# A fused window-attention, linear-attention and expert kernel: another order on all engines, three filler pairs per group instead of twelve

## The chip, the cores and the metric

The kernel runs on one core of a Trainium2 chip. The core has a matmul engine (PE, TensorE), three engines for the rest (DVE, VectorE; ACT, ScalarE; POOL, GpSimd) and SP, which issues DMAs. Each engine works through its own instructions in their order, and they wait for each other by semaphores. The metric is device microseconds of one execution, lower is better. Three runs of the kernel before took 11870.49, 11959.04 and 12028.54 us; the median is 11959.04.

## What is computed

The reference takes x of shape (32, 56, 56, 64) through three layers:

```python
x = _L0_conv_ref(x, ...)      # Swin block: LN, shifted 7x7 windows, 8 heads with bias and mask, projection,
                              # then LN, 64 -> 256 gelu, LN, 256 -> 64, both with residuals
t = _to_tokens(x)
t = t + _L1_attn_ref(_ln_t(t), ...)   # linear attention: k and v normed per head, kv = k^T v / HW,
                                      # q @ kv, projection, gelu, residual
t = t + _L1_ffn_ref(_ln_t(t), ...)    # softmax router, top 2 of 8 experts, 64 -> 256 gelu -> 64 each
```

## The kernel before, in words

The input is cut into 256 groups of 392 tokens (4 tiles of two 7x7 windows, 98 tokens each); eight groups make an image, over which the linear attention sums. Everything is one software pipeline. An iteration handles a different step of many groups at once: each engine has a list `ORDER[engine]` of `step:offset`, and in iteration n it executes the step for group n + offset. Offsets such as +2, +1, 0 belong to the window attention and its MLP, -1 to -2 to the linear attention's sums, -9 to -12 to its second pass and the router, and -24 to -27 to the experts. These work on tiles of 128 tokens that chose the same pair of experts; tokens are scattered to HBM by POOL and loaded again by SP, three tiles per iteration (271 iterations' worth). Behind the 256th group only the later offsets still run.

What a step name is on PE, with its line: `zT`, `oT`, `z2T`, `xnT`, `uT` four transposes each (L603); `q` L626, `k` L634, `v` L642; `s0` to `s3` attention scores of one tile (L650); `pT0` to `pT3` transposed probabilities (L658); `o0` to `o3` probabilities times values (L669); `proj` L683; `fc10`, `fc11` L695; `hT0`, `hT1` L704; `fc2` L714; `kv` L727; `G` L734; `lp` L766; `logit` L779; `rk` L787 to L791; `tx` L801; `ei0` to `ei2` the experts' first layer in f16 (L820); `eo0` to `eo2` their second layer (L829 the bias, L834). An f32 matmul shows as two records in the profile.

PE has eight banks of results, ps0 to ps7 (letters A, O, P, S, B, H, K, Y). Before a step writes a bank, `handed_on` waits until whoever read the bank's former content is done; the table `HANDED` holds, for each step, these signals in the order in which they can be expected.

A filler is a step whose name begins with f: `fK0`, `fP0` and so on, with the bank's letter. It is `keep_warm` (L609 to L615), two f16 matmuls of 128 x 512 whose results nobody reads:

```python
            def keep_warm(name, bank):
                handed_on(pe, name)
                for _ in range(2):
                    pe.matmul(bank[:, :], identh[:, :], we1[0][:, 0:512], start=True, stop=True)
```

They run only for the 256 groups, in `fK0 fP0 fS0 fK1 fY0 fA0 fK2 fS1 fB0 fY1 fP1 fH0`.

Of the kernel before, what the change touches and what calls it, by code (L numbers as in the profile page):

```python
# [80 lines left out]
def build(nc, x, cst, wqkv, bqkv, table, projw, projb, fc1w, fc1b, fc2w, fc2b, amask, rel, lnvecs, ln3,  # L81
# [12 lines left out]
    with ExitStack() as ctx:  # L94
# [263 lines left out]


        ORDER = dict(  # L360
            pe="""tx:-26 q:+2 fK0:+0 s0:+2 pT1:+1 o0:+1 s1:+2 z2T:+0 o1:+1 ei0:-26 lp:-10 fP0:+0 pT2:+1 mix0:+0 fc10:+0
                  mix1:+0 fS0:+0 s2:+2 ei1:-26 fc11:+0 mix2:+0 o2:+1 pT3:+1 xnT:-10 fK1:+0 mix3:+0 uT:-1 logit:-10 s3:+2
                  v:+2 hT0:+0 ei2:-26 fY0:+0 o3:+1 fA0:+0 hT1:+0 mix4:+0 fK2:+0 kv:-1 eo0:-26 oT:+1 fS1:+0 fB0:+0 eo1:-26
                  zT:+3 eo2:-26 proj:+1 fc2:+0 fY1:+0 fP1:+0 fH0:+0 k:+3 rk:-10 pT0:+2 G:-1""",
            dve="""u:-1 t2:-10 mix0:+0 oj0:+1 stx:-10 mix1:+0 mvx:-10 cx:-10 sa:-11 xn:-10 sb2:+2 mx1:+2 mix2:+0 rt0:-10
                   sb3:+2 c1:+3 tw:-11 rt1:-10 rt2:-10 z:+3 rt3:-10 st30:+0 mix3:+0 pa:-11 li:-11 rc0:+1 oj1:+1 mx2:+2
                   on0:+1 rc1:+1 rt4:-10 mx3:+2 rt5:-10 on1:+1 rt6:-10 st31:+0 rt7:-10 kvss:-1 rt8:-10 rt9:-10 mv1:+4
                   w:-11 mv3:+0 kve:-1 yv:-26 rt10:-10 rt11:-10 rt12:-10 kvr:-1 x1:+1 cd:-10 tr:+0 pk:-10 t:+0 st2:+1
                   kvn:-1 stu:+0 sl:-11 mv2:+1 Gsum:-1 c2:+1 sp:-10 qbd:+3 st1:+5 z2:+1 ya:-26 ct:-10 sb0:+3 ys:-26 sb1:+3
                   mx0:+3 mvu:+0 lo:-10 cu:+0""",  # L370
            act="""sd:-2 exp:+1 ke:+2 xc:-26 pt0:+1 pt1:+1 tanh:-11 om0:+1 z2t:+0 h00:-26 lpg:-10 pt2:+1 h01:-26 h02:-26
                   ge0:+0 h03:-26 h10:-26 utc:-9 ge1:+0 pt3:+1 xnt:-10 h11:-26 h12:-26 utk:-1 h13:-26 om1:+1 h20:-26
                   hi:-10 h21:-26 hnt0:+0 hnt1:+0 h22:-26 ve:+2 h23:-26 sq:-1 ot:+1 zt:+3""",
            pool="""pw3:-1 r2:+0 pw2:+0 r1:+3 ri:-27 sc0:-12 dm00:-12 dm10:-13 dm20:-14 dm30:-15 dm40:-16 dm50:-17
                    dm60:-18 x1b:+0 ru:-1 pwu:-1 pw1:+3 sc1:-12 dm01:-12 dm11:-13 dm21:-14 dm31:-15 dm41:-16 dm51:-17
                    dm61:-18 so0:-27 rx:-10 pwx:-10 sub0:+2 v0:-10 tu:-2 tk:-9 so1:-27 v1:-10 sc2:-12 dm02:-12 dm12:-13
                    dm22:-14 dm32:-15 dm42:-16 dm52:-17 dm62:-18 sub1:+2 sub2:+2 sc3:-12 dm03:-12 dm13:-13 dm23:-14
                    dm33:-15 dm43:-16 dm53:-17 dm63:-18 so2:-27 r3:+0 sub3:+2""",
            sp="""x:+6 tl:-25 tz:-25 ls:-12 wl:-24""",
        )  # L380

        HANDED = dict(
            fA0="uT_kept.0:-1 hid_ready.1:+0 z2T_ready.0:+0 q_ready.0:+2 x1_ready.0:+0 zT_ready.0:+2 oT_ready.0:+0 hnT_ready.1:-1",
            q="x1_ready.0:+0 zT_ready.0:+2 oT_ready.0:+0 hnT_ready.1:-1 uT_kept.0:-2 hid_ready.1:-1 z2T_ready.0:-1 q_ready.0:+1",
            z2T="q_ready.0:+2 x1_ready.0:+0 zT_ready.0:+2 oT_ready.0:+0 hnT_ready.1:-1 uT_kept.0:-2 hid_ready.1:-1 z2T_ready.0:-1",
            fc11="z2T_ready.0:+0 q_ready.0:+2 x1_ready.0:+0 zT_ready.0:+2 oT_ready.0:+0 hnT_ready.1:-1 uT_kept.0:-2 hid_ready.1:-1",
            uT="hid_ready.1:+0 z2T_ready.0:+0 q_ready.0:+2 x1_ready.0:+0 zT_ready.0:+2 oT_ready.0:+0 hnT_ready.1:-1 uT_kept.0:-2",
            hT1="uT_kept.0:-1 hid_ready.1:+0 z2T_ready.0:+0 q_ready.0:+2 x1_ready.0:+0 zT_ready.0:+2 oT_ready.0:+0 hnT_ready.1:-1",
            oT="hnT_ready.1:+0 uT_kept.0:-1 hid_ready.1:+0 z2T_ready.0:+0 q_ready.0:+2 x1_ready.0:+0 zT_ready.0:+2 oT_ready.0:+0",
            zT="oT_ready.0:+1 hnT_ready.1:+0 uT_kept.0:-1 hid_ready.1:+0 z2T_ready.0:+0 q_ready.0:+2 x1_ready.0:+0 zT_ready.0:+2",  # L390
            proj="zT_ready.0:+3 oT_ready.0:+1 hnT_ready.1:+0 uT_kept.0:-1 hid_ready.1:+0 z2T_ready.0:+0 q_ready.0:+2 x1_ready.0:+0",
            fB0="hnT_ready.0:+0 logit_ready.0:-10 xnT_ready.0:-10 hid_ready.0:+0 gelu_ready.0:-10 spot_ready.0+count_ready.0:-11 fc2_scaled.0:-1",
            lp="spot_ready.0+count_ready.0:-11 fc2_scaled.0:-1 hnT_ready.0:-1 logit_ready.0:-11 xnT_ready.0:-11 hid_ready.0:-1 gelu_ready.0:-11",
            fc10="gelu_ready.0:-10 spot_ready.0+count_ready.0:-11 fc2_scaled.0:-1 hnT_ready.0:-1 logit_ready.0:-11 xnT_ready.0:-11 hid_ready.0:-1",
            xnT="hid_ready.0:+0 gelu_ready.0:-10 spot_ready.0+count_ready.0:-11 fc2_scaled.0:-1 hnT_ready.0:-1 logit_ready.0:-11 xnT_ready.0:-11",
            logit="xnT_ready.0:-10 hid_ready.0:+0 gelu_ready.0:-10 spot_ready.0+count_ready.0:-11 fc2_scaled.0:-1 hnT_ready.0:-1 logit_ready.0:-11",
            hT0="logit_ready.0:-10 xnT_ready.0:-10 hid_ready.0:+0 gelu_ready.0:-10 spot_ready.0+count_ready.0:-11 fc2_scaled.0:-1 hnT_ready.0:-1",
            fc2="hnT_ready.0:+0 logit_ready.0:-10 xnT_ready.0:-10 hid_ready.0:+0 gelu_ready.0:-10 spot_ready.0+count_ready.0:-11 fc2_scaled.0:-1",
            rk="fc2_scaled.0:+0 hnT_ready.0:+0 logit_ready.0:-10 xnT_ready.0:-10 hid_ready.0:+0 gelu_ready.0:-10 spot_ready.0+count_ready.0:-11",
            fK0="g_ready.0:-2 kv_ready.0:-2 mix3:-1 mix2:-1 mix1:-1 mix0:-1",  # L400
            fK1="mix2:+0 mix1:+0 mix0:+0 g_ready.0:-2 kv_ready.0:-2 mix3:-1",
            fK2="mix3:+0 mix2:+0 mix1:+0 mix0:+0 g_ready.0:-2 kv_ready.0:-2",
# [14 lines left out]
            v="pT_ready.3:+1 pT_ready.2:+1 pT_ready.1:+1 pT_ready.0:+1 vexp_ready.0:+1",
            pT0="vexp_ready.0:+2 pT_ready.3:+1 pT_ready.2:+1 pT_ready.1:+1 pT_ready.0:+1",
            fS0="score_bias.1:+2 score_bias.0:+2 score_bias.3:+1 score_bias.2:+1",
            fS1="score_bias.3:+2 score_bias.2:+2 score_bias.1:+2 score_bias.0:+2",  # L420
# [1254 lines left out]
```

How the kernel before makes its waits and increments, by code:

```python
        def now(eng, name, n, t=0, alone=None):  # L282
            if isinstance(n, int) and (n < 0 or COUNTS[name] * n + t + 1 <= 0):
                return
            eng.wait_ge(S[name], COUNTS[name] * n + (t + 1))
            if alone:
                eng.sem_inc(held[alone], 1)
# [151 lines left out]
        def handed_on(eng, name):  # L441
            for entry in HANDED[name].split():
                signals, at = entry.split(":")
                at = int(at)
                if signals[:3] == "mix":
                    if runs_at("mix", ran["like"] + at, 0):
                        eng.wait_ge(mix_dve, 5 * (ran["image"] if ran["like"] % GROUPS + at >= 0 else ran["image"] - 1)
                                    + MIX_DONE[int(signals[3])])
                        return
                    continue
                parts = signals.split("+")
                last = STEPS if parts[0].split(".")[0] in ("xs_ready", "yv_ready", "h_ready") else TOTAL
                if ran["like"] + at in range(last):
                    for part in parts:
                        signal, t = part.split(".")
                        now(eng, signal, ran["n"] + at, int(t))
                    return
# [56 lines left out]
        @block.sync  # L516
        def _(sp):
            for dst, src in SETUP_LOADS:
                sp.dma_start(dst, src).then_inc(setup, 16)
            sp.wait_ge(setup_dve, 9)
            for w in range(2):
                sp.dma_start(pos[w * WA:(w + 1) * WA, :], pos1).then_inc(setup_pos, 16)
```

## Time and profile before

| | before |
|---|---|
| median of three runs | 11959.04 us (11870.49 to 12028.54) |
| the profiled execution | 11922.89 us, its span 11921.1 us |
| granted TensorE clock, mean of the span | 0.769 |
| PE busy | 10713.8 us, 90% |
| DVE, ACT, POOL busy | 6277.7, 5532.9, 5262.0 us |
| filler matmuls (L615) | 6144, 2237.0 us busy |

The busy time of PE counts from the start of a matmul to its modelled end, and matmuls overlap, so a busy PE is not PE at its peak. The granted clock is the share of TensorE's full 2.4 GHz; it has two levels here, 1.00 and 0.50, and a value between is a mean over both.

### The profile page before, as it was taken

How to read it: one execution, taken by the hardware profiler on the slowest of the kernel's cores; microseconds unless marked ns; L12 is line 12 of the kernel's file. 1: busy time of each engine (PE TensorE's matmuls, PEld its weight loads, DVE VectorE, ACT ScalarE, POOL GpSimd, SP SyncE). 2: the span in 40 equal slices, each digit the busy share in tenths (PEclk: the TensorE clock that was granted, in tenths of full speed). 3: DMA queues.
4: the chain of work that ended last, by engine and by line, in shares of the span. 5: the costliest groups of instructions: out<-in, count | busy, mean ns of one | idle time of the engine just before them, and what ended most of it. 6: DMA issues, size and time to landing. Idle time of an engine off the chain costs nothing. (4 is left out here: it accounts for less than half of the span.)

```text
span 11921.1 us, 262791 instructions
## 1 busy us (share of the span) xinstructions
PE 10713.8 (90%) x67913; PEld 7893.3 (66%) x67913; DVE 6277.7 (53%) x26878; ACT 5532.9 (46%) x12487; POOL 5262.0 (44%) x7260
## 2 busy tenths in 40 slices
PE   7899999999999999999999999999999999999655
PEld 5666666666666666666666667666666666666544
DVE  5666555555555565655555555555555555555200
ACT  3545444445544454544445454445445444454211
POOL 2444444444544444544444454444444444454321
PEclk9878777778877787877778787778878877787555
...
GB/s 20 7 9 14 14 16 16 15 15 16 17 15 15 15 16 16 16 16 16 15 16 16 16 16 16 15 16 17 16 16 16 16 16 15 16 16 14 21 19 10
DMA packets 222504, 184.37 MB, mean 15 GB/s; under 512 B 63337, under 2 KB 193331, under 8 KB 220552
## 3 DMA queue, kind: packets, MB, share of 16 engines
...
## 5 line engine op out<-in xcount | busy, mean ns | idle before, releaser
L615 PE MATMUL ps<-we_hi,identh 128*128 128x512 f16 x6144 | 2237.0, 477 | 36.9 <-DVE yv L1304 35.9
L1605 ACT ACTIVATE ht<-ps,be 128x128 f32<-128x128 f32 x3252 | 1109.7, 369 | 1212.7 <-PE ps L820 758.1
L1364 POOL TENSOR_TENSOR sc<-sc,mx 98x392 f32<-98x392 f32 x1024 | 860.3, 840 | 1756.4 <-DVE mx L1012 1743.6
...
L1427 POOL DMA_INDIRECT slots<-rec,slot x1024 | 1072.4, 1047 | 356.1 <-issue 225.2
L650 PE MATMUL ps<-kexp,qbd 128*98 128x392 f32 x2048 | 1134.7, 643 | 75.1 <-DVE qbd L999 52.8
L834 PE MATMUL ps<-we,ht 128*128 x6504 | 1181.5, 340 | 0.0
L834 PEld LDWEIGHTS ps<-we,ht 128*128 128x128 f32 x6504 | 1053.3, 246 | 132.1 <-issue 73.3
L1513 ACT ACTIVATE first<-ps,cs 98x144 f32<-98x144 f32 x512 | 194.6, 380 | 2020.7 <-PE ps L669 2020.7
L1454 POOL DMA_INDIRECT out_y<-ys,row_at x813 | 838.8, 1032 | 592.4 <-DVE ys L1316 245.9
L820 PE MATMUL ps<-xs,we_hi 128*128 128x128 f16 x3252 | 699.6, 251 | 405.9 <-issue 271.6
L669 PEld LDWEIGHTS ps<-vexp,pt 98*98 98x98 f32 x8192 | 974.7, 191 | 99.4 <-issue 28.6
L615 PEld LDWEIGHTS ps<-we_hi,identh 128*128 128x128 f16 x6144 | 663.8, 122 | 492.7 <-issue 254.3
L669 PE MATMUL ps<-vexp,pt 98*98 98x36 f32 x8192 | 955.1, 267 | 0.0
L1495 ACT ACTIVATE kexp<-ps,cs 128x196 f32<-128x196 f32 x2048 | 672.0, 440 | 478.5 <-PE ps L634 472.8
L695 PE MATMUL ps<-wf,z2t 65*98 65x256 f32 x2048 | 650.9, 447 | 252.4 <-ACT rec L1575 251.1
L1006 DVE TENSOR_TENSOR sc<-ps,bias 98x392 f32<-98x392 f32 x1024 | 574.6, 561 | 530.9 <-PE ps L650 530.2
L820 PEld LDWEIGHTS ps<-xs,we_hi 128*128 x3252 | 357.6, 110 | 724.5 <-issue 623.0
L1353 POOL TENSOR_TENSOR rs<-ve,cs 98x4 f32<-98x4 f32 x768 | 781.9, 1018 | 70.1 <-issue 49.6
L1480 ACT ACTIVATE pt<-ps 98x392 f32<-98x392 f32 x1024 | 514.1, 502 | 567.4 <-PE ps L658 560.4
L820 PE MATMUL ps<-xs,we_lo 128*128 128x128 f16 x3252 | 694.6, 244 | 0.4
L1097 DVE TENSOR_SCALAR kvse<-kvsd 98x128 f32<-98x128 f32 x256 | 58.6, 229 | 1177.7 <-ACT kvsd L1570 1177.7
...
## 6 DMA issues: line engine op xcount, KB each, us to landing
...
xg<-in_x SPq DMA_DIRECT2D x256, 98.0 KB
...
lw<-tile_list SPq DMA_DIRECT2D x271, 0.0 KB
...
tile_list<-entry SPq DMA_DIRECT2D x64, 0.5 KB
```

Of the source, the lines that this page charges most:

```text
L615: pe.matmul(bank[:, :], identh[:, :], we1[0][:, 0:512], start=True, stop=True)
L650: pe.matmul(pS[0:TOK, 0:HEADS * WA], qbd[:, t, :], kexp[:, t, :], start=True, stop=True)\
L669: last = pe.matmul(o[:, :, 2 * h:2 * h + 2, :], pt[:, t % 2, h, :], vexp[:, 2 * t:2 * t + 2, 2 * h:2 * h + 2, :], start=True, stop=True)
L695: last = pe.matmul((pB, pA)[half][0:TOK, (t % 2) * HID:(t % 2 + 1) * HID], z2t_[:, cols(t)], wf1[:, :], start=True, stop=True)
L820: last = pe.matmul(pH[:, 128 * (2 * e + h):128 * (2 * e + h + 1)], we1[half][:, bass.ds(pair[e] * HID + 128 * h, 128)], xs[:, q, :], start ...
L834: last = pe.matmul(dst, ht[:, q, 2 * e + h, :], we2[:, bass.ds(chosen[q][e] * 2 + h, 1), :].rearrange("p a c -> p (a c)"), start=False, st ...
L1353: pool.tensor_tensor(rs[L][:, :, :], ve[L][:, :, :], k("minushalf")[0:TOK].unsqueeze(1).to_broadcast([TOK, ve[L].shape[1], GT]), ALU.pow)\
L1364: pool.tensor_tensor(s, s, mx[:, t, :].unsqueeze(2).to_broadcast([TOK, HEADS, WA]), ALU.subtract)\
L1427: pool.indirect_dma_start(slots, bass.IndirectOffsetOnAxis(ap=slot[:, j % 2, t:t + 1], axis=0), rec[:, bass.ts(j % RB, 1), t, :].rearrange ...
L1454: pool.indirect_dma_start(out, bass.IndirectOffsetOnAxis(ap=row_at[:, q:q + 1], axis=0), ys[:, bass.ts(j % 2, 1), q, :].rearrange("p a c - ...
L1495: last = act.activation(kexp[:, :, WA * h:WA * (h + 1)], keys_, ACT.Copy, scale=k("headmask")[:, h:h + 1])
L1605: act.activation(ht[:, q, b, :], pH[:, 128 * b:128 * (b + 1)], ACT.Gelu, bias=be1[:, bass.ds(chosen[q][b // 2] * 2 + b % 2, 1)], scale=1.0 ...
```

## The change

Only the tables `ORDER` and `HANDED` are different. Nine of the twelve filler steps are gone (`fH0`, `fS0`, `fB0` stay), and the steps of all four computing engines stand in another order; some move to the neighbouring iteration, which changes their offset. No operation of the computation is added or removed. SP's list is the same. Lines below the tables stand 9 lines higher. Of the PE list and of HANDED:

```diff
-            pe="""tx:-26 q:+2 fK0:+0 s0:+2 pT1:+1 o0:+1 s1:+2 z2T:+0 o1:+1 ei0:-26 lp:-10 fP0:+0 pT2:+1 mix0:+0 fc10:+0
+            pe="""mix0:+0 tx:-26 fH0:+0 zT:+2 v:+1 mix1:+0 lp:-10 fS0:+0 q:+2 k:+2 pT0:+1 fB0:+0 rk:-11 z2T:+0 ei0:-26
...
-            fH0="h_ready.11:-26 h_ready.7:-26 h_ready.3:-26",
+            fH0="h_ready.11:-27 h_ready.7:-27 h_ready.3:-27",
```

The whole order on PE in an iteration is now: mix0 tx fH0 zT v mix1 lp fS0 q k pT0 fB0 rk z2T ei0 s0 pT1 mix2 fc10 fc11 o0 s1 ei1 o1 xnT mix3 s2 uT pT2 logit ei2 o2 hT0 pT3 kv hT1 o3 eo0 s3 eo1 eo2 mix4 oT fc2 proj G. It was: tx q fK0 s0 pT1 o0 s1 z2T o1 ei0 lp fP0 pT2 mix0 fc10 mix1 fS0 s2 ei1 fc11 mix2 o2 pT3 xnT fK1 mix3 uT logit s3 v hT0 ei2 fY0 o3 fA0 hT1 mix4 fK2 kv eo0 oT fS1 fB0 eo1 zT eo2 proj fc2 fY1 fP1 fH0 k rk pT0 G.

The first place on PE is behind fc2. In the kernel before (L714 is fc2, L615 the fillers, L634 k, L787 to L791 rk):

```order
L683 MATMUL ps<-wp,ot 98x64 x4
L714 MATMUL ps<-wf,hnt 98x64 x8
L615 MATMUL ps<-we_hi,identh 128x512 x6
L634 MATMUL ps<-zt,wa 64x196 x2
L787 MATMUL ps<-count,onesf 128x140
```

In the changed kernel (L705 is fc2, L674 proj, L725 G, L792 tx, L606 the filler pair fH0, L594 zT, L633 v):

```order
L705 MATMUL ps<-wf,hnt 98x64 x8
L674 MATMUL ps<-wp,ot 98x64 x4
L725 MATMUL ps<-kvn 65x65 x4
L287 ISA
L792 MATMUL ps<-identh,rt 128x128 x3
L606 MATMUL ps<-we_hi,identh 128x512 x2
L287 REGISTER_ALU
L594 MATMUL ps<-cs,z 64x98 x4
L633 MATMUL ps<-wa,zt 98x64 x8
```

Three filler pairs in a row became one, and it stands behind proj, G and tx.

The second place is around s0. In the kernel before (L626 q, L650 s0, L658 pT1, L669 o0):

```order
L801 MATMUL ps<-identh,rt 128x128 x3
L626 MATMUL ps<-zt,wq 64x196 x2
L615 MATMUL ps<-we_hi,identh 128x512 x2
L650 MATMUL ps<-kexp,qbd 98x392
L658 MATMUL ps<-cs,pr 98x98 x4
L669 MATMUL ps<-vexp,pt 98x2x18 x4
```

In the changed kernel, from the pair fB0 on (L778 to L782 rk, L594 z2T, then ei0, of which the first matmul is shown; its last, s0 (L641), pT1 and fc10 and fc11 (L686) follow behind the "..."):

```order
L606 MATMUL ps<-we_hi,identh 128x512 x2
L778 MATMUL ps<-count,onesf 128x140
L780 MATMUL ps<-pick,before 128x112
...
L594 MATMUL ps<-cs,z 64x98 x4
...
L811 MATMUL ps<-xs,we_lo 128x128
L641 MATMUL ps<-kexp,qbd 98x392
L649 MATMUL ps<-cs,pr 98x98 x4
L686 MATMUL ps<-wf,z2t 98x256 x4
```

No filler stands between q and s0 any more; rk, z2T and ei0 stand between the pair and s0.

## Rows read from the trace of the kernel before

**Rows 1.** The page: span, and busy time of each engine with its share and instructions.
```profile
span 11921.1 us, 262791 instructions
PE 10713.8 (90%) x67913; PEld 7893.3 (66%) x67913; DVE 6277.7 (53%) x26878; ACT 5532.9 (46%) x12487; POOL 5262.0 (44%) x7260
```

**Rows 2.** Busy time by stretch; L650's and L615's alone (PE, PEld, PEclk, DMA).
```profile
core 0: us, PE busy (x) PEld busy (x) DVE busy (x) ACT busy (x) POOL busy (x), PEclk, DMA share, GB/s
5000.00:7000.00 2000.00, 1865.37 (x11915) 1368.88 (x11914) 1109.94 (x4778) 973.05 (x2193) 926.81 (x1282) 0.78 0.06 16
11000.00:11921.00 921.00, 543.43 (x2621) 430.68 (x2620) 125.67 (x541) 182.48 (x588) 241.39 (x303) 0.50 0.07 17
...
5000.00:7000.00 2000.00, 203.73 (x368) 60.54 (x368) 0.78 0.06 16
...
11000.00:11921.00 921.00, 0.00 (x0) 0.00 (x0) 0.50 0.07 17
```

**Rows 3.** Single groups by stretch, from proj to proj (columns as in rows 2).
```profile
1108.00:1143.60 35.60, 32.25 (x263) 24.14 (x262) 23.53 (x100) 21.07 (x49) 20.52 (x29) 1.00 0.07 18
4066.90:4124.30 57.40, 53.30 (x263) 38.87 (x262) 23.57 (x100) 22.31 (x49) 19.88 (x28) 0.55 0.05 12
10314.10:10370.80 56.70, 53.27 (x262) 38.82 (x262) 23.59 (x100) 22.28 (x49) 19.91 (x28) 0.55 0.04 12
```

**Rows 4.** Waits, 5000 to 7000 us: who waited for whom, total, times, longest.
```profile
PE ps L695 <- ACT rec L1575: 46.2, 41, 1.2
PE ps L820 <- issue: 25.1, 27, 1.0
```

**Rows 5.** Timeline of PE: start, us, what; full level first, then low, then pairs.
```profile
6047.85 1.55 PE L714 MATMUL ps<-wf,hnt 128*98 128x64 f32 x16
6049.23 1.46 PE L615 MATMUL ps<-we_hi,identh 128*128 128x512 f16 x6
...
6013.08 2.77 PE L615 MATMUL ps<-we_hi,identh 128*128 128x512 f16 x6
...
6001.21 0.60 PE L615 MATMUL ps<-we_hi,identh 128*128 128x512 f16 x2
...
6054.76 1.03 PE L615 MATMUL ps<-we_hi,identh 128*128 128x512 f16 x2
```

**Rows 6.** Stretches around a fall of the clock (as rows 2), then PE's timeline there.
```profile
6003.40:6009.20 5.80, 5.80 (x44) 4.62 (x43) 3.65 (x21) 4.23 (x11) 3.29 (x6) 1.00 0.10 28
6009.40:6016.00 6.60, 6.60 (x32) 4.67 (x33) 5.18 (x24) 3.75 (x4) 0.65 (x1) 0.50 0.14 37
6016.20:6026.00 9.80, 9.16 (x82) 6.38 (x78) 6.12 (x24) 5.68 (x15) 5.49 (x9) 1.00 0.03 7
...
6007.82 0.48 PE L829 MATMUL ps<-b2pair,onesf 1*128 x2
6008.24 1.10 PE L834 MATMUL ps<-we,ht 128*128 x8
6009.18 1.44 PE L683 MATMUL ps<-wp,ot 65*98 65x64 f32 x8
6010.41 2.87 PE L714 MATMUL ps<-wf,hnt 128*98 128x64 f32 x16
```

**Rows 7.** L615 in 3 us before each rise; then all of those 355 us.
```profile
5989.20:5992.20 3.00, 1.06 (x2) 0.30 (x2) 0.50 0.10 28
...
6340.80:6343.80 3.00, 1.06 (x2) 0.17 (x2) 0.50 0.10 28
sum 36.00, PE 20.69 PEld 5.44; mean PE 1.72 PEld 0.45
...
5988.80:6343.80 355.00, 334.65 (x2100) 244.20 (x2098) 195.34 (x846) 171.25 (x388) 164.28 (x229) 0.77 0.06 16
```

**Rows 8.** A stretch at the low level: L615 in it, and its row behind fc2.
```profile
6111.70:6169.70 58.00, 12.03 (x24) 3.25 (x24) 0.50 0.06 14
...
6144.43 2.74 PE L615 MATMUL ps<-we_hi,identh 128*128 128x512 f16 x6 [1.26 <-DVE yv L1304]
```

More of the change, by code:

```diff
@@ L360, in build @@
         ORDER = dict(
-            pe="""tx:-26 q:+2 fK0:+0 s0:+2 pT1:+1 o0:+1 s1:+2 z2T:+0 o1:+1 ei0:-26 lp:-10 fP0:+0 pT2:+1 mix0:+0 fc10:+0
[L362 to L378, printed above, removed]
+            pe="""mix0:+0 tx:-26 fH0:+0 zT:+2 v:+1 mix1:+0 lp:-10 fS0:+0 q:+2 k:+2 pT0:+1 fB0:+0 rk:-11 z2T:+0 ei0:-26
+                  s0:+2 pT1:+1 mix2:+0 fc10:+0 fc11:+0 o0:+1 s1:+2 ei1:-26 o1:+1 xnT:-10 mix3:+0 s2:+2 uT:-1 pT2:+1
+                  logit:-10 ei2:-26 o2:+1 hT0:+0 pT3:+1 kv:-1 hT1:+0 o3:+1 eo0:-26 s3:+2 eo1:-26 eo2:-26 mix4:+0 oT:+1
+                  fc2:+0 proj:+1 G:-1""",
@@ new lines, in build @@
+            dve="""mix0:+0 tr:-1 mv2:+0 c2:+0 mix1:+0 cd:-11 t:-1 stu:-1 pk:-11 mvu:-1 qbd:+2 z2:+0 t2:-10 stx:-10 mvx:-10
+                   st1:+4 sp:-11 c1:+3 ct:-11 cx:-10 sa:-11 sb0:+2 xn:-10 cu:-1 tw:-11 mx0:+2 z:+3 mv1:+4 sb1:+2 st30:+0
+                   mix2:+0 mx1:+2 sl:-11 u:-1 w:-11 st31:+0 mv3:+0 rt0:-10 oj0:+1 rt1:-10 pa:-11 li:-11 rt2:-10 rc0:+1
+                   rt3:-10 mix3:+0 rt4:-10 sb2:+2 on0:+1 kvss:-1 mx2:+2 rt5:-10 rt6:-10 rt7:-10 rt8:-10 oj1:+1 sb3:+2
+                   rc1:+1 mx3:+2 rt9:-10 kve:-1 on1:+1 rt10:-10 lo:-10 kvr:-1 yv:-26 kvn:-1 ya:-26 x1:+1 Gsum:-1 rt11:-10
+                   st2:+1 ys:-26 rt12:-10""",
@@ new lines, in build @@
+            act="""om1:+0 hnt1:-1 sd:-2 ot:+0 exp:+1 xc:-26 zt:+2 tanh:-11 ve:+1 lpg:-10 ke:+2 pt0:+1 z2t:+0 h00:-26
+                   utc:-9 h01:-26 pt1:+1 h02:-26 ge0:+0 h03:-26 h10:-26 h11:-26 ge1:+0 xnt:-10 om0:+1 h12:-26 h13:-26
+                   utk:-1 pt2:+1 hi:-10 h20:-26 hnt0:+0 h21:-26 pt3:+1 h22:-26 h23:-26 sq:-1""",
+            pool="""ri:-27 sub3:+1 pw3:-1 sc0:-12 dm00:-12 dm10:-13 dm20:-14 dm30:-15 dm40:-16 dm50:-17 dm60:-18 tu:-3
+                    r2:+0 pw2:+0 so0:-27 sc1:-12 dm01:-12 dm11:-13 dm21:-14 dm31:-15 dm41:-16 dm51:-17 dm61:-18 ru:-1
+                    rx:-10 pwx:-10 pwu:-1 tk:-11 r1:+4 v0:-10 sc2:-12 dm02:-12 dm12:-13 dm22:-14 dm32:-15 dm42:-16
+                    dm52:-17 dm62:-18 sub0:+2 so1:-27 v1:-10 r3:+0 sc3:-12 dm03:-12 dm13:-13 dm23:-14 dm33:-15 dm43:-16
+                    dm53:-17 dm63:-18 pw1:+4 so2:-27 sub1:+2 x1b:+0 sub2:+2""",
@@ L382, in build @@
         HANDED = dict(
[L383 to L402, printed above, removed]
+            zT="x1_ready.0:+0 oT_ready.0:+0 hnT_ready.1:-1 uT_kept.0:-2 hid_ready.1:-1 z2T_ready.0:-1 q_ready.0:+1 zT_ready.0:+1",
@@ new lines, in build @@
+            q="zT_ready.0:+2 x1_ready.0:+0 oT_ready.0:+0 hnT_ready.1:-1 uT_kept.0:-2 hid_ready.1:-1 z2T_ready.0:-1 q_ready.0:+1",
+            z2T="q_ready.0:+2 zT_ready.0:+2 x1_ready.0:+0 oT_ready.0:+0 hnT_ready.1:-1 uT_kept.0:-2 hid_ready.1:-1 z2T_ready.0:-1",
+            fc11="z2T_ready.0:+0 q_ready.0:+2 zT_ready.0:+2 x1_ready.0:+0 oT_ready.0:+0 hnT_ready.1:-1 uT_kept.0:-2 hid_ready.1:-1",
+            uT="hid_ready.1:+0 z2T_ready.0:+0 q_ready.0:+2 zT_ready.0:+2 x1_ready.0:+0 oT_ready.0:+0 hnT_ready.1:-1 uT_kept.0:-2",
@@ new lines, in build @@
+            hT1="uT_kept.0:-1 hid_ready.1:+0 z2T_ready.0:+0 q_ready.0:+2 zT_ready.0:+2 x1_ready.0:+0 oT_ready.0:+0 hnT_ready.1:-1",
+            oT="hnT_ready.1:+0 uT_kept.0:-1 hid_ready.1:+0 z2T_ready.0:+0 q_ready.0:+2 zT_ready.0:+2 x1_ready.0:+0 oT_ready.0:+0",
+            proj="oT_ready.0:+1 hnT_ready.1:+0 uT_kept.0:-1 hid_ready.1:+0 z2T_ready.0:+0 q_ready.0:+2 zT_ready.0:+2 x1_ready.0:+0",
+            fB0="gelu_ready.0:-10 fc2_scaled.0:-1 hnT_ready.0:-1 logit_ready.0:-11 xnT_ready.0:-11 hid_ready.0:-1 spot_ready.0+count_ready.0:-12",
@@ new lines, in build @@
+            lp="fc2_scaled.0:-1 hnT_ready.0:-1 logit_ready.0:-11 xnT_ready.0:-11 hid_ready.0:-1 spot_ready.0+count_ready.0:-12 gelu_ready.0:-11",
+            rk="gelu_ready.0:-10 fc2_scaled.0:-1 hnT_ready.0:-1 logit_ready.0:-11 xnT_ready.0:-11 hid_ready.0:-1 spot_ready.0+count_ready.0:-12",
+            fc10="spot_ready.0+count_ready.0:-11 gelu_ready.0:-10 fc2_scaled.0:-1 hnT_ready.0:-1 logit_ready.0:-11 xnT_ready.0:-11 hid_ready.0:-1",
+            xnT="hid_ready.0:+0 spot_ready.0+count_ready.0:-11 gelu_ready.0:-10 fc2_scaled.0:-1 hnT_ready.0:-1 logit_ready.0:-11 xnT_ready.0:-11",
@@ L403, in build @@
+            logit="xnT_ready.0:-10 hid_ready.0:+0 spot_ready.0+count_ready.0:-11 gelu_ready.0:-10 fc2_scaled.0:-1 hnT_ready.0:-1 logit_ready.0:-11",
+            hT0="logit_ready.0:-10 xnT_ready.0:-10 hid_ready.0:+0 spot_ready.0+count_ready.0:-11 gelu_ready.0:-10 fc2_scaled.0:-1 hnT_ready.0:-1",
+            fc2="hnT_ready.0:+0 logit_ready.0:-10 xnT_ready.0:-10 hid_ready.0:+0 spot_ready.0+count_ready.0:-11 gelu_ready.0:-10 fc2_scaled.0:-1",
             mix0="g_ready.0:-2 kv_ready.0:-2 mix3:-1 mix2:-1 mix1:-1 mix0:-1",
@@ L408, in build @@
             G="kv_ready.0:-1 mix3:+0 mix2:+0 mix1:+0 mix0:+0 g_ready.0:-2",
+            k="o_joined.1:+0 o_joined.0:+0 kexp_ready.0:+1",
             o0="kexp_ready.0:+2 o_joined.1:+0 o_joined.0:+0",
             o2="o_joined.0:+1 kexp_ready.0:+2 o_joined.1:+0",
-            k="o_joined.1:+1 o_joined.0:+1 kexp_ready.0:+2",
-            fP0="pT_ready.1:+1 pT_ready.0:+1 vexp_ready.0:+1 pT_ready.3:+0 pT_ready.2:+0",
-            fP1="vexp_ready.0:+2 pT_ready.3:+1 pT_ready.2:+1 pT_ready.1:+1 pT_ready.0:+1",
+            v="pT_ready.3:+0 pT_ready.2:+0 pT_ready.1:+0 pT_ready.0:+0 vexp_ready.0:+0",
+            pT0="vexp_ready.0:+1 pT_ready.3:+0 pT_ready.2:+0 pT_ready.1:+0 pT_ready.0:+0",
             pT1="pT_ready.0:+1 vexp_ready.0:+1 pT_ready.3:+0 pT_ready.2:+0 pT_ready.1:+0",
@@ L416, in build @@
             pT3="pT_ready.2:+1 pT_ready.1:+1 pT_ready.0:+1 vexp_ready.0:+1 pT_ready.3:+0",
[L417 to L420, printed above, removed]
+            fS0="score_bias.3:+1 score_bias.2:+1 score_bias.1:+1 score_bias.0:+1",
             s0="score_bias.3:+1 score_bias.2:+1 score_bias.1:+1 score_bias.0:+1",
@@ L424, in build @@
             s3="score_bias.2:+2 score_bias.1:+2 score_bias.0:+2 score_bias.3:+1",
-            fY0="xs_ready.0:-26 yv_ready.0:-27",
-            fY1="yv_ready.0:-26 xs_ready.0:-26",
             tx="yv_ready.0:-27 xs_ready.0:-27",
             eo0="xs_ready.0:-26 yv_ready.0:-27",
-            fH0="h_ready.11:-26 h_ready.7:-26 h_ready.3:-26",
+            fH0="h_ready.11:-27 h_ready.7:-27 h_ready.3:-27",
             ei0="h_ready.11:-27 h_ready.7:-27 h_ready.3:-27",
```

## The prediction

> **What bounds the kernel now.** I read the page first, then the steady stretch, then single groups. The page [rows 1] gives 11921.1 us of span, PE busy 90% of it, DVE 53%, ACT 46%, POOL 44%. From about 1000 to 11000 us the kernel repeats one pattern: [rows 2] show 368 score matmul records (L650, 8 for a group) in 2000 us, so 46 groups, 43.5 us for a group, at a granted clock of 0.78. Behind 11000 us only the experts' tail is left (921 us), at 0.50.
>
> That 0.78 is a mean of two levels: 1.00 is 2.4 GHz, 0.50 is 1.2 GHz. I write s for the share of time at the full level; 0.78 is s = 0.57. [rows 3] put single groups beside each other, cut from one `proj` (L683) to the next. At clock 1.00 a group takes 35.6 us; at 0.55 (s = 0.10) two of them take 57.4 and 56.7 us. In these low groups PE is busy 53.3 us, DVE 23.6, ACT 22.3, POOL 19.9: nobody but PE is near the bound. Even in the full group the others have 12 us to spare (23.5, 21.1, 20.5 of 35.6), while PE is busy 32.3. So PE sets the pace at both levels, and what a group costs is PE's work divided by its clock. The waits between engines [rows 4] are small on PE: the longest, fc1 behind the gelu on ACT, is 46.2 us in 46 groups, 1.0 us each.
>
> **The change, part by part.** Three things happen: 18 of 24 filler matmuls (L615) go from each group; all steps stand in another order; the waits that went with the fillers go with them.
>
> *Fillers.* Six of them in a row take 1.46 us at the full level and two take 0.60 [rows 5], so one costs (1.46 - 0.60) / 4 = 0.215 us. At the low level six take 2.77 and two 1.03: (2.77 - 1.03) / 4 = 0.435 us. Eighteen are 3.9 us at full and 7.8 us at low. They write banks that are overwritten and nobody reads; DVE, ACT and POOL lose nothing. At the low level all of the 7.8 us is on the path, since PE is busy 93% there. At full, up to the same 3.9 us; if the fillers only covered waits that now open, as little as 0.
>
> *The new order.* The same operations on each engine; every step of a group is still there. On PE I looked for a step put right behind the one it waits for. fc2 now stands between oT and proj and covers the copy of ot; z2T has ei0, s0 and pT1 before fc10; v uses the zT of a group before. No place looks worse than the one of now. I cost the reordering at 0 us, with 1.0 us for a group either way (the longest PE wait of [rows 4] taken away or doubled), 250 us over the run.
>
> *Were the clock to stay as it is*, that would be all: at s = 0.57 about 0.57 x 3.9 + 0.43 x 7.8 = 5.6 us less for a group if all counts.
>
> *The clock.* It does not stay by itself: what PE executes decides it. In [rows 6] PE has no idle time at all from 6003.4 to 6009.2 us, at 1.00, and still the clock is 0.50 from 6009.4 on. What PE does there are the experts' second layer (L829, L834), two transposes (L603), then proj: many weight loads with 64 to 98 columns each, and bias matmuls with one active row. Then six fillers run at the low level, and from 6016.2 us the clock is 1.00 again. The same stretch of steps one group later, 6045 to 6051 [rows 5], stayed at full.
>
> How the clock comes back is shown by [rows 7]: I took the 3 us before each of the 12 rises between 5989 and 6344 us. Every one holds fillers: five hold six of them, one four, six two; the fillers are busy 20.69 of the 36 us. The stretch that never rose is as telling: 58 us from 6111.7 to 6169.7 at 0.50, with all 24 fillers in it [rows 8]; its triple came behind a wait of 1.26 us on yv. The pairs that stand alone beside transposes or small matmuls did not lift the clock.
>
> In the new order there is no triple and no double any more (the first pair of order pieces in the section on the change): fc2 is followed by proj, G and tx, then one pair. Nor does a pair stand directly beside a score matmul (s) or an expert's first layer (ei), as fK0 before s0, fS0 before s2 and fY0 behind ei2 do now (the second pair of pieces shows the first of them): rk and z2T stand between fB0 and ei0. What is left that is dense in full-size matmuls is one place: ei0 followed directly by s0.
>
> The Trainium skill (TensorE: Matmul & The Clock Gate, section "Why this matters for your kernels") puts it as a matter of idle gaps: keep TensorE busy without gaps between bursts and it keeps its clock. By that rule, with PE nearly as busy after the change as now, the clock would stay, and the time would be that of the third rival below. The trace disagrees: the drop of rows 6 falls into a stretch without any gap. The same page says in its Part 4 that transposes do not count as activity in the way of other matmuls; that fits the drop, and it speaks against an order in which transposes and small matmuls stand alone.
>
> **The sum.** One line through the groups. Low: the mean of 57.4 and 56.7 is 57.05 at s = 0.10; full: 35.6 at s = 1. Slope (57.05 - 35.6) / 0.9 = 23.8, so 59.4 us at s = 0. After: 59.4 - 7.8 = 51.6 at s = 0 and 35.6 - 3.9 = 31.7 at s = 1, or P = 51.6 - 19.9 s. The line gives 45.8 for the kernel of now at s = 0.57, where 43.5 was measured: it lies up to 2.3 us high in the middle and little near the ends. Break-even with 43.5 is at s = 0.41, a granted clock of 0.70.
>
> What is s after? Now: 12 rises in 355 us, 8.2 groups, so 1.5 rises for a group; at clock 0.77, s = 0.54 [rows 7], the full stretches are 355 x 0.54 / 12 = 16 us long each. After: none of the 12 had a filler-free cover, and one moderately dense place for a group is left. I take one rise in two groups (my choice, between 0 and 1), and stretches of 14 us, a bit shorter, since the fillers that carried PE over its waits are gone. s = 0.5 x 14 / 49 = 0.14, granted clock 0.57. P = 51.6 - 2.8 = 48.8; half a microsecond off for the line's bulge: 48.3. That is 4.8 us more than 43.5, on about 250 groups (256, the first few run in the ramp): +1200 us. The ramp before and the tail behind have the same work, and the tail has no fillers [rows 2]: 0. The last is 11921 + 1200 = 13120; with what lies around the span (11922.89 against 11921.1) and the roundings I say **13100 us**. The profiled execution is 0.3% under the median of the runs shown (11959.04), within their spread of 11870 to 12029.
>
> **Rivals.**
> - *The clock stays almost always low* (s under 0.05): the one dense place is not enough. P = 51.6 to 50.6, say 51.3: +7.8 x 250 = 1950, 13,870 us. For it: the stretch of 58 us in rows 8 with all its fillers. Chance 0.18.
> - *The clock falls only to about 0.70* (s = 0.36 to 0.46): nearly two rises for a group in stretches of 10 us. P near 43.5, 11,650 to 12,150 us, no change. Chance 0.08.
> - *Faster: the clock stays where it is.* Were s 0.57, P = 51.6 - 11.3 = 40.3 by the line and 43.5 - 5.6 = 37.9 by subtraction; 11,921 - 250 x 3.2 = 11,120 down to 10,520 us. It decides from s = 0.46 on. The mechanism would be that s and ei, with 128 active rows each, hold the clock by themselves. For it: the group keeps all eight s records of 392 columns and 24 ei matmuls of 128. Against it: [rows 6, 7]. Chance 0.09. The Trainium skill's rule on idle gaps (page and section as above) would have it so too.
> - *The waits open.* At full, the fillers covered waits, so 3.9 us come back as idle. At s = 0.14 that is 0.14 x 3.9 = 0.5 us for a group, +140 us; it moves nothing by itself, but idle PE time at full makes the next fall earlier. It is in the upper half of the forecast's range.
>
> **The numbers.** Forecast (s between 0.05 and 0.36) 0.65, always low 0.18, same 0.08, faster 0.09. A change of 2% is about what a measurement of this kernel can tell from no change (its three runs lie 1.3% apart). Slower by over 2%: 0.83; same 0.08; faster 0.09. The range leaves out faster, same and the far end of low: from s = 0.33 (P = 45.0, +1.5 x 250 = 380: 12,300 us) to s near 0 (P = 51.4, +7.9 x 250 = 1980: 13,900 us).
>
> **What would show it.** In the profile after, the steady stretch should have PE still over 90% busy, a granted clock of 0.52 to 0.62, fewer groups in 2000 us (about 41 instead of 46), L615 with a quarter of its records, and stretches of 50 us and more at 0.50. Fillers at full should still cost 0.215 us each. DVE, ACT and POOL should have the same busy time for a group. If the clock is at 0.75 or above, the step on the clock is wrong and the kernel is faster; if it is at 0.55 and the group takes over 52 us, the new order has waits at the low level that I costed at 0; if the group at full takes over 34 us, the fillers covered waits.

## The result and the profile after

The changed kernel takes 12502.32 us (median of 4 runs, 12440.77 to 12611.87) against 11952.26 us of the kernel before beside it: a ratio of 1.047, 95% interval 1.036 to 1.058. It is slower, as forecast, and inside the range of 12,300 to 13,900 us; but the forecast was 13,100, +1200 us for the span, and the span grew by 12454.0 - 11921.1 = 533 us. The size was wrong by more than a factor of two. The ratios and their intervals, here and in the table of experiments, leave out executions that took over 1.5% more than the fastest of the same kernel; the medians are of all.

The page of the changed kernel, span and busy time of each engine, beside [rows 1]:

```profile
span 12454.0 us, 253288 instructions
PE 11746.4 (94%) x63305; PEld 9438.6 (76%) x63305; DVE 6529.8 (52%) x26878; ACT 5623.8 (45%) x12487; POOL 5294.9 (43%) x7260
```

PE has 4608 matmuls less and is busy 1033 us longer. Its steady stretch, then two groups from proj to proj, then PE's stretches around one rise and one fall (busy time by stretch, columns as in [rows 2]):

```profile
5000.00:7000.00 2000.00, 1960.42 (x10683) 1578.99 (x10683) 1110.73 (x4586) 951.84 (x2106) 894.65 (x1229) 0.60 0.06 15
2960.30:3009.60 49.30, 49.30 (x244) 40.16 (x243) 27.68 (x115) 22.01 (x49) 20.34 (x28) 0.50 0.05 14
4836.10:4880.80 44.70, 43.72 (x245) 35.32 (x244) 24.16 (x100) 21.71 (x49) 20.37 (x28) 0.61 0.06 15
4880.80:4898.00 17.20, 17.20 (x95) 13.06 (x95) 9.35 (x51) 9.77 (x22) 7.19 (x10) 0.52 0.02 5
4898.20:4908.20 10.00, 9.12 (x71) 6.76 (x69) 7.14 (x31) 4.39 (x13) 5.75 (x9) 0.97 0.05 16
4908.80:4925.00 16.20, 16.20 (x75) 14.19 (x74) 7.72 (x19) 6.37 (x12) 7.03 (x9) 0.50 0.11 25
```

The granted clock of the steady stretch is 0.60 where it was 0.78. A group wholly at 1.2 GHz takes 49.3 us, in all of which PE is busy; a common group takes 44.7 us and holds one piece of some 10 us at 2.4 GHz. The timeline of PE shows where that piece begins and ends. At the low level stand ei0 (L811) and directly behind it s0 (L641); the transposes pT1 (L649) behind them are already faster (0.72 us; 0.50 is the full level). Towards the end stand logit (L770) and a gap before ei2 (L811). The matmuls of ei2 still take 0.22 to 0.23 us; o2 (L660) and hT0 (L695) behind it are slow again:

```profile
4895.32 0.31 PE L811 MATMUL ps<-xs,we_hi 128*128 128x128 f16 x1
4895.43 0.31 PE L811 MATMUL ps<-xs,we_lo 128*128 128x128 f16 x1
4895.54 1.57 PE L641 MATMUL ps<-kexp,qbd 128*98 128x392 f32 x2
4896.90 0.72 PE L649 MATMUL ps<-cs,pr 98*98 98x98 f32 x4
...
4903.95 0.50 PE L594 MATMUL ps<-cs,u 98*64 98x98 f32 x4 [0.35 <-ACT hid L1534]
4904.28 0.50 PE L649 MATMUL ps<-cs,pr 98*98 98x98 f32 x4
4904.71 0.85 PE L770 MATMUL ps<-wrt,xnt 64*98 64x8 f32 x8
4906.07 0.23 PE L811 MATMUL ps<-xs,we_hi 128*128 128x128 f16 x1 [0.50 <-issue]
...
4907.20 1.17 PE L660 MATMUL ps<-vexp,pt 98*98 98x36 f32 x8
4908.17 0.90 PE L695 MATMUL ps<-cs,hid 98*128 98x98 f32 x4
```

No filler pair stands at either end of this piece. The trace says how common it is: of 134 rises between 1000 and 9000 us, 118 have ei0 directly followed by s0 in the 3 us before them, and 130 of 133 falls have the ei2 behind logit there. The three pairs are almost never near a rise: in 9 of the 134 the pair fH0 stands in those 3 us, in the others none. PE's waits, by place (5000 to 7000 us: total, times, longest), are the counterpart of [rows 4]:

```profile
PE ps L811 <- issue: 16.1, 34, 0.6
PE ps L594 <- ACT hid L1534: 10.7, 31, 0.4
PE ps L792 <- issue: 7.4, 6, 1.5
```

The wait of fc1 for the gelu, 46.2 us before, is gone, and no wait of that size took its place.

### The profile page after: what moved, and what is told of

It is laid out like the page before. It is cut to its first block and busy times, and to the rows that moved or that the text cites. A ratio compares the mean times of both kernels' runs of the same rounds, so it can differ in the third digit from the quotient of the medians.

```text
span 12454.0 us, 253288 instructions
## 1 busy us (share of the span) xinstructions
PE 11746.4 (94%) x63305; PEld 9438.6 (76%) x63305; DVE 6529.8 (52%) x26878; ACT 5623.8 (45%) x12487; POOL 5294.9 (43%) x7260
## 5 line engine op out<-in xcount | busy, mean ns | idle before, releaser
L825 PE MATMUL ps<-we,ht 128*128 x6504 | 1582.6, 424 | 0.0
L825 PEld LDWEIGHTS ps<-we,ht 128*128 128x128 f32 x6504 | 1430.9, 324 | 180.2 <-issue 177.7
L641 PE MATMUL ps<-kexp,qbd 128*98 128x392 f32 x2048 | 1317.4, 738 | 12.0 <-issue 6.9
L660 PEld LDWEIGHTS ps<-vexp,pt 98*98 98x98 f32 x8192 | 1166.1, 228 | 112.1 <-issue 38.3
L660 PE MATMUL ps<-vexp,pt 98*98 98x36 f32 x8192 | 1181.5, 302 | 23.0 <-DVE first L1011 9.3
L811 PE MATMUL ps<-xs,we_hi 128*128 128x128 f16 x3252 | 767.7, 268 | 358.6 <-issue 199.2
L649 PEld LDWEIGHTS ps<-cs,pr 98*98 98x98 f32 x4096 | 597.5, 180 | 334.2 <-issue 334.0
L811 PEld LDWEIGHTS ps<-xs,we_hi 128*128 x3252 | 378.9, 117 | 618.0 <-issue 509.3
L606 PE MATMUL ps<-we_hi,identh 128*128 128x512 f16 x1536 | 791.9, 617 | 6.6 <-ACT rec L1566 6.6
L649 PE MATMUL ps<-cs,pr 98*98 98x98 f32 x4096 | 774.0, 334 | 0.0
L811 PE MATMUL ps<-xs,we_lo 128*128 128x128 f16 x3252 | 753.1, 262 | 2.0
L705 PE MATMUL ps<-wf,hnt 128*98 128x64 f32 x4096 | 714.3, 365 | 0.0
L705 PEld LDWEIGHTS ps<-wf,hnt 128*98 128x98 f32 x4096 | 707.4, 288 | 0.0
```

Source lines behind the costliest of these rows:

```text
L641: pe.matmul(pS[0:TOK, 0:HEADS * WA], qbd[:, t, :], kexp[:, t, :], start=True, stop=True)\
L649: last = pe.transpose(pP[0:TOK, cols(h)], pr[:, t, TOK * h:TOK * (h + 1)], ident[0:TOK, 0:TOK])
L660: last = pe.matmul(o[:, :, 2 * h:2 * h + 2, :], pt[:, t % 2, h, :], vexp[:, 2 * t:2 * t + 2, 2 * h:2 * h + 2, :], start=True, stop=True)
L705: last = pe.matmul(pB[0:TOK, C * t:C * (t + 1)], hnt[:, t, h, :], wf2[:, h, :], start=(h == 0), stop=(h == 1))
L811: last = pe.matmul(pH[:, 128 * (2 * e + h):128 * (2 * e + h + 1)], we1[half][:, bass.ds(pair[e] * HID + 128 * h, 128)], xs[:, q, :], start ...
L825: last = pe.matmul(dst, ht[:, q, 2 * e + h, :], we2[:, bass.ds(chosen[q][e] * 2 + h, 1), :].rearrange("p a c -> p (a c)"), start=False, st ...
```

## The experiments

All run beside the kernel before (its medians there: 11967 to 12004 us). Steady clock is the granted clock of 5000 to 7000 us; a group is 2000 us divided by the number of groups in them (score matmul records by 8). That is one sample and can be off by up to 1 us: from 1500 to 9000 us the mean is 43.6 us before, 45.7 in the changed kernel and 37.9 in after_3moved. Where a run adds, drops or moves pairs, `HANDED` has the entries that these need, and nothing else differs.

| kernel | order | pairs | median us | ratio, 95% interval | steady clock | group us |
|---|---|---|---|---|---|---|
| before | old | 12 | 11952 | 1 | 0.78 | 43.5 |
| before_12moved | old | 12, places of after_12pairs | 13385 | 1.120 (1.111 to 1.129) | 0.70 | 48.8 |
| before_3pairs | old | 3 | 12812 | 1.066 (1.058 to 1.075) | 0.62 | 46.5 |
| after | new | 3 | 12502 | 1.047 (1.036 to 1.058) | 0.60 | 45.5 |
| after_s0_late | new | 3 | 12610 | 1.050 (1.043 to 1.057) | 0.58 | |
| after_0pairs | new | 0 | 12049 | 1.011 (1.007 to 1.015) | 0.59 | 43.2 |
| after_3moved | new | 3, other places | 10671 | 0.893 (0.888 to 0.898) | 0.76 | 37.0 |
| after_4pairs | new | 4 | 11384 | 0.951 (0.944 to 0.959) | 0.68 | 41.2 |
| after_12oldplaces | new | 12, places of before | 10114 | 0.852 (0.836 to 0.867) | 0.92 | 35.7 |
| after_7pairs | new | 7 | 9905 | 0.830 (0.826 to 0.835) | 0.91 | 34.3 |
| after_9pairs | new | 9 | 9789 | 0.824 (0.810 to 0.838) | 0.91 | 34.5 |
| after_12pairs | new | 12 | 9662 | 0.806 (0.801 to 0.811) | 0.97 | 33.5 |

**Only the pairs taken away, old order.** `before_3pairs`:

```diff
-            pe="""tx:-26 q:+2 fK0:+0 s0:+2 ... ei0:-26 lp:-10 fP0:+0 pT2:+1 ... proj:+1 fc2:+0 fY1:+0 fP1:+0 fH0:+0 k:+3
+            pe="""tx:-26 q:+2 s0:+2 ... ei0:-26 lp:-10 pT2:+1 ... proj:+1 fc2:+0 fH0:+0 k:+3
```

> The order of the kernel before, with only the pairs fH0, fS0 and fB0 of its twelve; nothing else moves. Theory (the fillers set the clock): the granted clock of the steady stretch falls from 0.78 to about 0.60 as in the changed kernel, because only fS0 beside s2 and ei1 still lifts it once in a group; the old order has its own waits on PE (fc1 behind gelu, 1.0 us for a group), so 12500 to 12900 us. Rival (the new order is what costs): little changes but 18 fillers less, 11000 to 11900 us.

Measured 12812 us, clock 0.62: as the clock theory has it. The fillers taken away cost 7%, not the order. What the order is worth is shown by a group wholly at the low level, with the same three pairs as the changed kernel:

```profile
2480.50:2532.80 52.30, 50.53 (x244) 39.86 (x244) 23.59 (x100) 20.02 (x47) 19.89 (x28) 0.50 0.06 14
...
2491.29 1.62 PE L641 MATMUL ps<-kexp,qbd 128*98 128x392 f32 x2 [0.91 <-DVE qbd L990]
2501.76 2.03 PE L686 MATMUL ps<-wf,z2t 65*98 65x256 f32 x4 [0.84 <-ACT rec L1566]
```

52.3 us against 49.3 us: the new order takes 3.0 us less for a group, 0.91 + 0.84 = 1.75 us of it two waits (s0 for qbd, fc1 for gelu) that it does not have. In the rest PE is busy longer for the same 244 matmuls (50.53 against 49.30 us); why is not shown, nor which of the four engines' lists brings the gain, since they changed together.

**No pair at all, new order.** `after_0pairs`:

```diff
-            pe="""mix0:+0 tx:-26 fH0:+0 zT:+2 v:+1 mix1:+0 lp:-10 fS0:+0 q:+2 k:+2 pT0:+1 fB0:+0 rk:-11 z2T:+0 ei0:-26
+            pe="""mix0:+0 tx:-26 zT:+2 v:+1 mix1:+0 lp:-10 q:+2 k:+2 pT0:+1 rk:-11 z2T:+0 ei0:-26 s0:+2 pT1:+1 mix2:+0
```

> The changed kernel without its three pairs. Theory: those three pairs stand in the low stretches and never lift the clock (it rises behind ei0 and s0, which stay), so the clock stays near 0.60, a group loses 6 x 0.43 = 2.6 us, and the run takes 11850 to 12050 us, about the time of the kernel before with no filler at all. Rival (the clock follows the number of fillers): the clock goes to 0.50 to 0.53 and the run takes 12300 to 12500 us.

Measured 12049 us, clock 0.59: the three pairs that the change keeps hold next to nothing. Without them a group is 45.5 - 43.2 = 2.3 us shorter by the table, and a group wholly at the low level 49.3 - 46.8 = 2.5 us, near their price of 2.6:

```profile
2024.50:2071.30 46.80, 46.80 (x239) 39.50 (x237) 23.69 (x100) 21.76 (x49) 20.78 (x28) 0.50 0.07 14
```

The rival that the number of fillers sets the clock falls here.

**Is ei0 followed by s0 the only place?** `after_s0_late`:

```diff
-                  s0:+2 pT1:+1 mix2:+0 fc10:+0 fc11:+0 o0:+1 s1:+2 ei1:-26 ...
+                  pT1:+1 mix2:+0 fc10:+0 s0:+2 fc11:+0 o0:+1 s1:+2 ei1:-26 ...
```

> The changed kernel with one step moved on PE: s0 stands behind pT1 and fc10, no longer directly behind ei0. Same work. Theory (ei0 directly followed by s0 is the only place that lifts the clock): no rise is left, granted clock 0.50 to 0.52, 49.5 us for a group, 13300 to 13550 us. Rival (the place means nothing, the mean load of PE sets the clock): 12400 to 12550 us.

Missed: 12610 us and a clock of 0.58; the forecast of no rise at all was wrong, and so was the word "only". The time lies 60 us over the range of the rival (the mean load sets the clock) and 690 us under that of the theory, so this run by itself speaks for the rival; what speaks against it is `after_3moved` below. The clock now rises elsewhere, as here behind s2 (L641) between two sets of transposes, with ei1 just before (by stretch, then PE's timeline):

```profile
3244.00:3250.60 6.60, 6.60 (x33) 4.90 (x33) 3.66 (x15) 2.34 (x7) 3.55 (x6) 0.50 0.06 15
3251.40:3256.00 4.60, 4.58 (x52) 4.25 (x50) 1.92 (x9) 3.11 (x10) 3.61 (x4) 1.00 0.05 13
...
3247.13 1.49 PE L660 MATMUL ps<-vexp,pt 98*98 98x36 f32 x8
3248.43 0.84 PE L594 MATMUL ps<-cs,xn 98*64 98x98 f32 x4
3249.07 1.51 PE L641 MATMUL ps<-kexp,qbd 128*98 128x392 f32 x2
3250.38 0.86 PE L594 MATMUL ps<-cs,u 98*64 98x98 f32 x4
```

Of 83 rises between 1000 and 9000 us, 44 come behind s2 and 38 behind tx, the pair fH0, zT and v. Full stretches are fewer and longer here (14.1 us on average, against 134 of 11.4 us). So when the first place is taken away, others do most of its work, and the pair fH0, which stands near 9 of the 134 rises in the changed kernel, may count there. Which matmuls lift the clock by how much stays open, that of the transposes too.

**The new order with twelve pairs.** `after_12pairs`; each new pair in the bank of the step behind it, with that step's waits:

```diff
+                  ... ei0:-26 fS1:+0 s0:+2 ... mix3:+0 fS2:+0 s2:+2 uT:-1 pT2:+1 fB1:+0 logit:-10 fH2:+0 ei2:-26 ...
+                  ... fK1:+0 kv:-1 hT1:+0 o3:+1 fY0:+0 eo0:-26 ... mix4:+0 fA1:+0 oT:+1 fB2:+0 fc2:+0 proj:+1 fK2:+0 G:-1
```

> The order of the changed kernel with nine more pairs: before s0, s2, logit, ei2, kv, eo0, oT, fc2 and G, each in the bank of the step that it stands before. Theory: the clock rises in several places of a group and holds through logit and ei2, where it falls now; granted clock 0.80 to 0.90, 37 to 41 us for a group, 10400 to 11400 us, faster than the kernel before because the order has fewer waits on PE. Rival (the new order itself is worse than the old): 12000 us or more at the same clock as before, 0.78.

Measured 9662 us, 19.4% faster than the kernel before with the same number of fillers, and better than I expected. Steady stretch, and one group:

```profile
5000.00:7000.00 2000.00, 1941.38 (x15495) 1467.04 (x15494) 1494.20 (x6198) 1253.86 (x2849) 1224.74 (x1661) 0.97 0.08 20
...
4900.00:4932.10 32.10, 31.79 (x262) 24.07 (x261) 24.30 (x100) 21.05 (x50) 21.24 (x30) 1.00 0.08 21
```

At full a group takes 32.1 us against 35.6 of [rows 3] with as many fillers: 3.5 us is what the new order, with the pairs at its own places, saves at full. The clock falls only 30 times between 1000 and 9000 us (228 times in the kernel before), and 26 of these falls come with a wait of tx for loaded tiles, up to 6.2 us. The kernel before has this wait too. In 2000 us, here and then before:

```profile
PE ps L801 <- issue: 38.5, 7, 6.2
...
PE ps L801 <- issue: 20.9, 6, 6.1
```

**Order or places?** `before_12moved` and `after_12oldplaces` complete a square of two orders and two sets of places (ten of the old places are kept in the second; the double fS1 fB0, behind oT in the kernel before, is split into one pair before oT and one before fc2):

```diff
+            pe="""tx:-26 fH1:+0 fS2:+0 q:+2 fS3:+0 s0:+2 ... lp:-10 pT2:+1 mix0:+0 fc10:+0 mix1:+0 fS4:+0 s2:+2 ...
...
+                  ... ei0:-26 fK0:+0 s0:+2 ... xnT:-10 fK1:+0 mix3:+0 fS0:+0 s2:+2 uT:-1 fP0:+0 pT2:+1 logit:-10 ei2:-26
+                  fY0:+0 o2:+1 ... mix4:+0 fS1:+0 oT:+1 fB0:+0 fc2:+0 fY1:+0 fP1:+0 fH0:+0 proj:+1 G:-1
```

> The order of the kernel before with twelve pairs, moved to the places that they have in the changed order with twelve pairs (behind tx, before q, s0, s2, logit, ei2, kv, eo0, oT, fc2, rk and G). Same work as before. It divides the gain of 2300 us between the order of the steps and the places of the fillers. Theory A (the places count): 0.90 or more granted clock, 9800 to 10600 us. Theory B (the old order's waits on PE, 3 us for a group against under 1 us in the new one, throw the clock down whatever the places): granted clock 0.75 to 0.82, 11500 to 12200 us.

> The order of the changed kernel with twelve pairs, standing at the places that they had in the kernel before: before s0, pT2, s2, hT1, kv, oT and fc2, behind xnT and ei2, and three in a row behind fc2. With the run before_12moved it completes the square of two orders by two sets of places. Theory A (the new order, with PE's waits under 1 us for a group, holds the clock wherever twelve pairs stand): granted clock 0.88 or more in the steady stretch, 9650 to 10300 us. Theory B (the new order needs a pair at logit and ei2, where this one has none): granted clock 0.75 to 0.85, 10300 to 11500 us.

Old order: 11952 us with its own places, 13385 with the new ones. New order: 9662 with its own, 10114 with the old ones. Both theories of the first run were too kind: theory B had the clock hardly change, and the run lost 12% at 0.70. The wait of fc1 for the gelu, which the pair fP0 stood before, now stands alone behind lp and pT2, and PE has a second long wait, a filler for fs (PE's waits of before_12moved, then of after_12oldplaces):

```profile
PE ps L695 <- ACT rec L1575: 63.7, 41, 1.6
PE ps L615 <- DVE fs L1069: 24.1, 21, 1.9
...
PE ps L787 <- ACT rec L1575: 32.7, 43, 0.8
PE ps L820 <- issue: 18.9, 40, 0.7
```

In before_12moved 160 of the 181 falls between 1000 and 9000 us have the wait of fc1 as PE's longest in the 3 us before them (57 of 228 in the kernel before). No run put a pair back there alone, so the cause is read from the trace and not tested. The second run answered with theory A (0.92, 10114 us); 163 of its 225 falls stand at the wait of rk (L787), before which after_12pairs has a pair and this run none. So the order is worth 1840 us with the old places and 3720 us with the new ones, and a good place for a filler seems to be one next to a wait or a thin stretch of its own order.

**Three pairs at other places.** `after_3moved`, the same work as the changed kernel:

```diff
-            pe="""mix0:+0 tx:-26 fH0:+0 zT:+2 v:+1 mix1:+0 lp:-10 fS0:+0 q:+2 ...
+            pe="""mix0:+0 tx:-26 zT:+2 v:+1 mix1:+0 lp:-10 q:+2 ... mix3:+0 fS2:+0 s2:+2 uT:-1 pT2:+1 logit:-10 fH2:+0 ei2:-26
```

> The changed kernel with its three pairs, two of them moved on PE: from behind tx and before q, where the clock is low, to before s2 and before ei2, where it falls (logit and the wait behind it). Same work. Theory (a pair is worth what it holds, not that it runs): full stretches become longer than the 12 us of the changed kernel, about 20 us, share of full clock 0.35 to 0.5 instead of 0.20, 39 to 43 us for a group, 11000 to 11800 us. Rival (the number of pairs sets the clock): 12400 to 12600 us.

10671 us, 14.6% under the changed kernel (10671 / 12502) with nothing but two pairs moved, and below the range I gave. Its steady clock is 0.76, and its full stretches are 19.0 us long on average (about 20 was expected, 11.4 in the changed kernel). The work is the same, so neither the number of pairs nor the mean load sets the clock: this is the plainest evidence that the place decides.

**One pair more, four more, six more.** `after_4pairs` adds the pair before ei2, `after_7pairs` also those before logit, eo0 and fc2, `after_9pairs` also those before s0 and s2:

```diff
+                  ... logit:-10 fH2:+0 ei2:-26 ...
...
+                  ... pT2:+1 fB1:+0 logit:-10 fH2:+0 ei2:-26 ... o3:+1 fY0:+0 eo0:-26 ... oT:+1 fB2:+0 fc2:+0 ...
...
+                  ... ei0:-26 fS1:+0 s0:+2 ... mix3:+0 fS2:+0 s2:+2 ...
```

> The changed kernel with one pair more, before ei2, where the full stretch ends in most groups. Theory: the fall goes to the next weak place (the experts' second layer before fc2), full stretches of 18 to 22 us, share 0.35 to 0.5, 11000 to 11900 us. If the clock stays in that pass behind fc2 too, it holds for several groups and the time is under 10500 us. Rival (the number of pairs sets the clock): +0.4 us for a group at most, 12400 to 12700 us.

> The changed kernel with four pairs more: before logit, ei2, eo0 and fc2. Theory: the clock holds for whole groups as with twelve pairs (0.97 there), and a group at full needs 5 x 0.43 = 2.2 us less of fillers than with twelve, so 9100 to 9700 us. Rival (twelve are needed): granted clock 0.75 to 0.85, 10000 to 11000 us.

> The changed kernel with nine pairs: its three, the four of the run with seven (before logit, ei2, eo0, fc2), and the two before s0 and s2, which bring the clock back. A group at full should take 31 us (between 30.8 with seven and 32.1 with twelve). Theory: with s0 and s2 strengthened the clock returns within half a group after the wait that throws it down once in some eight groups, share of full clock 0.90 or more, 9350 to 9650 us, the fastest. If the pairs before kv, oT and G are what holds the clock with twelve, it stays at 0.82 and takes 9800 to 10000 us.

11384, 9905 and 9789 us. One pair, 0.43 us of work at full level and 0.87 at low, buys 1118 us of the run, within the range given. Seven hold the clock at 0.91 and a group at full takes 30.8 us, 1.3 us less than with twelve:

```profile
4000.00:4030.80 30.80, 29.47 (x247) 22.52 (x246) 23.65 (x99) 20.84 (x48) 20.04 (x28) 1.00 0.10 21
```

The run with seven came out 205 us over its range, the one with nine 139 us over. The pairs before s0 and s2 did not bring 0.95; the other branch of that expectation came near (the full share stays at 0.82, which is the 0.91 of the table, and 9800 us). Twelve stay the fastest though their full group is longer, because 0.97 against 0.91 is worth more than 1.3 us. Which of the pairs before kv, oT and G does that was not tried, but the traces point to oT. Without a pair there, 45 of the 77 falls with seven pairs, and 49 of the 87 with nine, come with its wait for on as PE's longest in the 3 us before; with twelve pairs none does (in after_7pairs, 5000 to 7000 us):

```profile
PE ps L598 <- DVE on L1028: 9.9, 15, 1.1
```

## Why the prediction was right in direction and wrong in size

- *PE sets the pace at both levels.* Right: in the low group after, PE is busy 49.30 of 49.3 us; in the full group of after_12pairs 31.79 of 32.1.
- *Fillers cost 0.435 us at low.* Right: three pairs cost 2.5 us in a group at the low level (49.3 against 46.8 in after_0pairs), against 2.6.
- *The clock falls when the fillers go, by what stands densely on PE.* Right: 0.60 in the steady stretch (0.52 to 0.62 was forecast, 0.57 its centre), and before_3pairs shows the same fall in the old order. That ei0 followed by s0 would be the place that lifts it was right too; that it is the one place was not (after_s0_late).
- *The drop of [rows 6].* My list of what PE does before it left out four fillers that stand in it and end 3 us before the proj that is slow; so fillers nearby did not keep the clock:

```profile
6005.08 1.03 PE L615 MATMUL ps<-we_hi,identh 128*128 128x512 f16 x4
```

- *How often it rises.* I chose one rise in two groups with 14 us each, s = 0.14. The trace has 0.77 rises for a group with 11.4 us each, and the steady 0.60 is s = 0.20. The choice rested on no count, so that the clock came out inside 0.52 to 0.62 was in part luck. By my own line, 0.06 more in s is 19.9 x 0.06 = 1.2 us less for a group.
- *The new order costs 0, within 1.0 us for a group.* **This is the term that failed.** It saves 3.0 us for a group at low (52.3 against 49.3 with the same pairs) and, with twelve pairs at other places, 3.5 us at full (35.6 against 32.1). I had read the old order's waits in [rows 4] (fc1 behind gelu, 1.0 us for a group) and listed what in the new order stands between a step and its need, but only to see that nothing got worse; I did not take the old waits off the sum. The line P = 51.6 - 19.9 s was built from old groups and carried them along: a group at the low level was to take 51.6 us and took 49.3. These 2.3 us are the 3.0 less 0.7 by which the line lay too low for the old order (51.6 against 52.3).
- *The line's bulge.* I took 0.5 us off for it. From the measured low group the line fits without it: 49.3 - 19.9 x 0.20 = 45.3, and 45.5 was measured.
- *The sum.* P was forecast at 48.3 us. Less 2.3 by the low level's price, less 1.2 by s, plus the 0.5 of the bulge, it is 45.3; measured were 45.5. On 250 groups the difference of 2.8 is 700 us, and the span was missed by 666 (13,120 against 12,454). The order's 2.3 us are the largest part.
- *The rival with the clock staying* did not come, and the rival with the clock always low neither. *The waits open* fell, for the new order: with seven pairs a group at full takes 30.8 us, less than the 31.7 that I had given to three, though 1.33 us of it are idle.
- *The Trainium skill's rule on idle gaps* (TensorE: Matmul & The Clock Gate, section "Why this matters for your kernels"), which I set beside the sum as a rival, does not describe this kernel: the low group of the changed kernel has no idle PE time at all and stays at 0.50 for 49.3 us.

So the slowdown is a loss and a gain. Taking the pairs away at the old order costs 860 us (12812 against 11952); the new order gives back 310 us (12502). That is less than 3.0 us on 250 groups would be; the rest was not taken apart, except that its clock is a little lower (0.60 against 0.62).
